# Cross attention of a decoder layer: the product of the maxima ahead of bank 0's in five of sixteen rounds, and the rows' statistics in round 11

## The reference

```python
x = x + _L0_xattn_ref(_layernorm(x, axis=-1), ctx_2048, Wq, bq, Wk, bk, Wv, bv, Wo, bo)
# b = 32, channels 128, 512 positions, 8 heads of 16 channels
q = _apply_rotary(q_emb, split_heads(_proj(x, Wq, bq)))
k = _apply_rotary(k_emb, split_heads(_proj(c, Wk, bk)))
v = split_heads(_proj(c, Wv, bv))
scores = jnp.einsum('bhtc,bhsc->bhts', q, k) / math.sqrt(K_CH)
p_attn = jax.nn.softmax(scores, axis=-1)
out = jnp.einsum('bhts,bhsc->bhtc', p_attn, v)
return _proj(out, Wo, bo)
```

## Time and profile before

| | us |
|---|---|
| median of 3 runs | 3923.88 |
| lowest and highest | 3922.64 and 3927.17 |
| the profiled execution | 3921.74 |
| its span, first to last instruction | 3919.9 |
| PE busy | 3775.1 (96%) |
| DVE busy | 2853.0 (73%) |
| ACT busy | 2340.5 (60%) |
| POOL busy | 1806.4 (46%) |
| mean granted clock of PE | 0.987 |

### The profile page before, as it was taken

One profiled execution on the slowest core, in us unless ns is written; L12 is line 12 of the kernel. 1 busy time (PEld: TensorE's weight loads), 2 busy tenths in 40 slices (PEclk: granted clock), 3 DMA queues, 4 the chain that ended last, 5 costly groups with the idle time before them and its releaser, 6 DMA issues.

```text
span 3919.9 us, 74126 instructions
## 1 busy us (share of the span) xinstructions
PE 3775.1 (96%) x24778; PEld 2974.5 (76%) x24778; DVE 2853.0 (73%) x5969; ACT 2340.5 (60%) x5418; POOL 1806.4 (46%) x2121
## 2 busy tenths in 40 slices
PE   7999999979999999999889999999999999999999
PEld 6888888844444444444389999999999999999998
DVE  5777777657888888888746777777777777877333
ACT  5777777647777777776725555555555555555221
POOL 2222223233555555554424556665666665665210
PEclk9999999979999999999999999999999999999999
DMA  5000000023443333444236999999999999998421
GB/s 203 20 26 23 23 23 23 18 79 109 126 124 121 122 123 122 128 133 143 85 102 197 270 260 267 268 267 264 259 268 267 265 267 267 268 267 235 157 94 60
DMA packets 290168, 621.37 MB, mean 159 GB/s; under 512 B 70000, under 2 KB 78576, under 8 KB 289664
## 3 DMA queue, kind: packets, MB, share of 16 engines
q1 hardware_dynamic: 224640, 464.01, 36.3%
q0 software_dynamic: 64000, 150.52, 15.9%
q10 hardware_dynamic: 1152, 2.10, 0.1%
HBM read 459.93 MB, written 155.98 MB: 157 GB/s over the span
## 4 chain that ended last, share of the span: by engine, by line
PE 85%; DVE 7%; ACT 4%; issue 3%; DMA 1%; SPq 1%; POOL 0%; DVEq 0%; ACTq 0%; POOLq 0%
PE ps L525 20%; PE ps L527 18%; PE ps L526 18%; PE ps L701 6%; PE ps L512 4%; PE ps L662 4%; PE ps L684 4%; PE ps L551 3%; PE ps L624 3%; PE ps L795 2%; PE ps L821 2%; ACT PX L973 2%; DVE WD L1454 1%; DVE NM L1306 1%; PE ps L543 1%
## 5 line engine op out<-in xcount | busy, mean ns | idle before, releaser
L525 PE MATMUL ps<-WG,XT 128*128 128x352 f32 x2304 | 765.4, 332 | 8.0 <-DVE XT L1483 5.4
L526 PE MATMUL ps<-WG,XT 128*128 128x352 f32 x2304 | 744.0, 323 | 0.0
L527 PE MATMUL ps<-WG,XT 128*128 128x352 f32 x2304 | 743.9, 323 | 0.0
L973 ACT ACTIVATE PX<-ps 128x1024 f32<-128x1024 f32 x512 | 523.4, 1022 | 261.1 <-PE ps L684 253.7
L1306 DVE TENSOR_REDUCE NM<-ps 128x2 f32<-128x1024 f32 x512 | 622.5, 1218 | 69.3 <-PE ps L662 65.9
L1800 POOL DMA_INDIRECT sum<-YO,TI x224 | 399.2, 1782 | 495.8 <-issue 392.0
L1447 DVE TENSOR_TENSOR WG<-WL,WG 128x704 fp32r<-128x704 f32 x528 | 450.2, 883 | 30.9 <-ACT WG L1086 30.7
L1119 ACT ACTIVATE HS<-ps 128x352 f32<-128x352 f32 x288 | 133.9, 465 | 559.5 <-PE ps L527 559.5
L1489 DVE TENSOR_TENSOR HS<-ps,HS 128x352 f32<-128x352 f32 x288 | 151.0, 524 | 423.6 <-ACT HS L1119 420.1
L525 PEld LDWEIGHTS ps<-WG,XT 128*128 128x128 f32 x2304 | 433.9, 188 | 9.1 <-DVE XT L1483 6.3
L906 ACT ACTIVATE PA<-ps,nb 128x128 f32<-128x128 f32 x1024 | 360.4, 381 | 131.7 <-DVE nb L1175 131.6
(11 more groups left out here) (275 smaller groups left out, 8677.5 us busy)
## 6 DMA issues: line engine op xcount, KB each, us to landing
WL<-in_w_gate SPq DMA_DIRECT2D x128, 704.0 KB, 4.3
WL<-in_w_up SPq DMA_DIRECT2D x128, 704.0 KB, 5.9
DL<-in_w_down SPq DMA_DIRECT2D x128, 512.0 KB, 8.4
kq_parts<-HL SPq DMA_DIRECT2D x64, 512.0 KB, 3.0
KS<-kq_parts SPq DMA_DIRECT2D x384, 64.0 KB
QS<-kq_parts SPq DMA_DIRECT2D x384, 64.0 KB
DL<-in_w_down SPq DMA_DIRECT2D x128, 192.0 KB, 9.1
CB<-sum POOLq DMA_DIRECT2D x64, 256.0 KB, 3.0
```

What stands on the lines that cost most here:

```text
L525: pe.matmul(out_, lh(0), rh(0), start=first, stop=False)
L526: pe.matmul(out_, lh(0), rh(1), start=False, stop=False)
L527: return pe.matmul(out_, lh(1), rh(0), start=False, stop=last)
L973: act.activation(PX[:, n % 4, :, :], ps[:, 5 * 512:7 * 512], ACT.Exp, scale=0.25).then_inc(S["a_px"], 1)
```

## The change

A tuple `FIRST` names five rounds: 0, 11, 12, 13 and 14. In these, `top(n)` stands ahead of the step on bank 0; in the others behind it, as before. This holds for PE (the product) and DVE (the reduction) alike. And `stats_m(b + 2)` is called in round 11, as its first step behind the round's products, and no longer in round 9 ahead of `stack`. Nothing is computed differently, and no wait is added or removed.

```diff
+FIRST = (0, 11, 12, 13, 14)
...
     if 0 <= n - LAG < 16 * NB:
         do("score", n - LAG)
+    if r in FIRST and 0 <= n < 16 * NB:
+        do("top", n)
     do(*{0: ("keys_of", b, 0), 1: ("maxima", b - 1, 1), 2: ("rotate", b + 1, 0, 0), 3: ("rotate", b + 1, 0, 1),
...
-    if 0 <= n < 16 * NB:
+    if r not in FIRST and 0 <= n < 16 * NB:
         do("top", n)
...
     if r == 9:
         do("high", b + 1, 1)
         do("low", b + 1, 1)
-        do("stats_m", b + 2)
         do("stack", b + 1, 0, 0)
...
     if r == 11:
+        do("stats_m", b + 2)
         do("away", b + 1, 1)
```

## The result

| | kernel before | changed kernel |
|---|---|---|
| median (lowest to highest) | 3926.47 us (3922.64 to 3927.58), 6 runs | 3940.22 us (3935.45 to 3950.07), 6 runs |
| profiled execution, span | 3921.74 us, 3919.9 us | 3940.55 us, 3938.7 us |
| mean granted clock over the span | 0.987 | 0.984 |

The changed kernel is slower: the ratio is 1.0041, with a 95% interval of 1.0027 to 1.0055. Forecast were 3931.1 us, within 3920 to 3939.

A forecast was written before the change was run, and what follows sets the result against it. TensorE was taken to bound the cross-attention block. Profiled 3921.74 us plus 29 blocks at +.25 us (7.3) gave 3929.0; with 2.1 for the median over the profiled run, 3931.1 us, range 3920 to 3939.

The forecast's parts named there:

- X11: `turn_g` of round 11 on TensorE: starts .43 us later because `top` of round 11 now stands ahead of it.
- T13 to G: Spacing on TensorE from `top` of round 13 to `gate`, start to start: .33 us.
- S13 to the `apply` of round 1: TensorE from `score` of round 13 to round 1's `apply`: bound by its own work, .18 us shorter.
- the pause before S13: TensorE stands .5 us before `score` of round 13, waiting for the exponential on ScalarE; before the change .2.
- TensorE's waits for PX: TensorE's waits for the exponential's output, summed over the blocks: up by about 9 us.
- XB's wait: VectorE's wait for `join`'s product: falls from 1.8 us to under .6, worth nothing on TensorE.
- The rule on mode changes: Score of round 13 to round 1's `apply`: 12 tiling-mode changes become 11, .10 us for one; kernel about 3933.4 us.
- What comes back from S13 on: From `score` of round 13, TensorE regains part of the .43 us delay: .18, leaving +.25 per block.
- 3921.74 + 7.3: Whole kernel: profiled time before plus 29 blocks (3 to 31) at .25 us each, giving 3929.0 us.
- Rival 1: Full-width products behind a pair (`gate`, `join`, `keys_of`) need .10 more: +.55 us per block, 3939.8 us, chance .20.
- Rival 2: ScalarE isn't late, round 12's exponential keeps its place: block .28 us shorter, 3915.8 us, chance .07.
- Rivals 3 and 4: VectorE bounds some rounds, 3914.4 us, chance .04; a later TensorE wait for ScalarE swallows the .25, 3923.9, chance .12.

The follow-up runs named there:

- e2: Changed kernel with the old order in every round, only the statistics still moved to round 11: 3928.54 us, ratio .9999 to the kernel before.
- e4: Changed kernel with `top` first in round 11 alone: 3951.00 us, ratio 1.0052 to the kernel before.
- e3: Changed kernel with round 11 taken out of the list, `top` first in 0, 12, 13 and 14: 3925.18 us, ratio .9992 to the kernel before.
- e7: Changed kernel with the copy to OS (`high_o`, with `low_o`) moved from round 11 to 12: 3924.25 us, ratio .9997 to the kernel before.
- e8: Kernel before with the copy to OS (`high_o`, with `low_o`) moved from round 11 to 12: 3921.37 us, ratio .9988.
- e9: Changed kernel without round 11 in the list and with the copy to OS in round 12: 3921.25 us, ratio .9983 to the kernel before.
- e10: As e9, and `high`/`low` of (b + 1, 1) moved from round 9 to 10: 3916.63 us, ratio .9976 to the kernel before.
- e6: Changed kernel with the new order only in blocks 0 to 2 and 28 to 31: 3929.16 us, ratio 1.0011 to the kernel before.
- e11: Changed kernel with `top`'s two products issued three times in round 12 to fill TensorE's pause: 3938.01 us, ratio 1.0032 to the kernel before.
- e12: Changed kernel with the new order only from block 1 on: 3936.72 us, ratio 1.0028 to the kernel before.
- e13: Changed kernel with the new order only from block 3 on: 3937.19 us, ratio 1.0031 to the kernel before.
- e14: As e10, with the new order only from block 3 on: 3914.42 us, ratio .9971 to the kernel before.
- after_again: Changed kernel measured once more without an edit, in a second group: 3937.86 us, ratio 1.0035 to the kernel before.

## Why the prediction was wrong, point by point

**Right, with its size:** what bounds the block. X11 slips by .44 (forecast .43), T13 to G is .33, G to A 1.01, S13 to the `apply` of round 1 9.24 (forecast 9.24), the pause before S13 .46 to .49 (forecast .5), the period +.245 (forecast +.25). TensorE's waits for PX rose by 12.9 us, where I had said about 9, because the whole .46 is new in the view: S13 had no recorded wait before (the pair ahead of it is drawn up to its start), and 29 x .46 = 13.3. XB's wait fell under .6 (23 of at most .4); six others come to 3.4 together, the longest 1.7. norm_m follows PX of round 13 without a gap. The statistics are worth nothing (e2).

**The rule on mode changes.** What comes back from S13 on was .18 (34.72 in e4, 34.54 in the changed kernel) and not .10: a pair behind a pair lasts .40 against .50, and what stands behind it starts .33 against .43 later. The Trainium skill, "TensorEngine Tiling (Array Packing)", Key Properties, is right that a change of mode costs, but counting the changes at .10 each gives too little back here; its estimate, 3933.4 us, is nearer to the measured time for a reason that has nothing to do with it.

**The step that failed** is the first sentence of the sum: 3921.74 + 7.3. It takes everything outside the 29 blocks' mechanism, the granted clock above all, as unchanged, and so puts blocks 0 to 2, where the order changes too, at nothing. Three things were missing from it.
1. The base. The median of the kernel before over six runs is 3926.47, not 3923.88; in the other groups it lay from 3925.65 to 3928.69. That is 2.6 of the 9.1 us between forecast and result, and no matter of the change.
2. The clock. It is .984 and .987 in the two profiled executions. Over all executions of this study (the kernel before, the changed one and 14 more) a line through time and mean clock, with a constant for each kernel, has a slope of 2.3 us for each .001. The mean clock of the changed kernel's 12 executions is .0011 to .0018 lower than before's, which gives 2.5 to 4 us. Part of it is the longer time at 1.2 GHz in blocks 0 to 2, shown in eleven traces above (2.6 and 2.9 us in the changed kernel's two).
3. At equal clock, by the same line, the changed kernel stands 8.0 and 11.0 us (its two groups) above the kernel before, some 9.5, and the blocks account for 7.1. About 2 us are not assigned.

The second group's median, 3937.86, lies inside the forecast's range, and the first lies 1.2 us outside, less than the two differ. So that the range was just missed is in part chance; that 5 to 7 us beyond the block's 7.1 were missing is not: the lower ends of the two intervals are 10.6 and 9.0 us.

My views were the stretch 1200 to 1600, where the clock is 1.00. The clock of the first 40 us and of the last 200 us of cross attention would have shown that the time isn't the block's period times the blocks: .66 and .97 there.

**The rivals.** Rival 1 named 3939.8, .4 from the measured median. It is refuted all the same: its deciding point was T to G above .38, and that is .33, in the changed kernel and in e3; its +.55 per block is .245. A number that fits is no evidence for its cause. Rival 2 (ACT isn't late) falls by the 1.08 us that ACT idles before x3T, and by e7. Rivals 3 and 4 fall by the period. The chances had .46 for a time within .2% and .43 for a slower one; slower came. A range that ended at 3939 left no room for an unpriced term of several us on top of the forecast.

**The expectations of the experiments** held for every block period to .05 but e8's (34.11 expected, 34.00 measured). They missed in whole times, in both directions: e4 (more lost, by dips in the clock), e3, e7, e9 and e10 (less gained), e6 (3.5 us lost, where the block gave 1 and the rival at least 5), e11 (no gain), e12 (no cure), e13 (a cure at the head, none of the whole), e14 (12 us gained of 13 to 15).

**What stays open.** Why the new order in blocks 0 to 2 brings more time at 1.2 GHz; why the pause before S13 is followed by a dip in some blocks and not in others (after_again has one in the middle, the first profiled execution none); whether the dips near the end belong to a kernel or to a run; the 2 us above. In the changed kernel's first profiled execution one standstill near the end remains without a cause:

```profile
1907.97 1.06 PE L705 MATMUL ps<-PX,vh 128*32 128x512 f32 x8
...
1909.84 0.63 PE L516 MATMUL ps<-CST,ox 128*128 128x128 f32 x4 [0.80 <-issue]
1910.37 1.02 ACT L977 ACTIVATE PX<-ps 128x1024 f32<-128x1024 f32 x1 [3.04 <-remote]
```

ACT idles 3.04 us before an exponential whose product had started at 1907.55, and nothing in the profile names what it waited for.

## What to carry to other kernels

When a step moves on the busiest engine, follow its reader through the in-order engine behind it: here the price of one pair put ahead was set by a copy that stood in ScalarE's queue between two others, and moving that copy was worth more than any order on TensorE. An idle stretch of an engine that nobody waits for is not a gain to be had, however large its number. And a sum of block periods is only a forecast of the time if the granted clock at the ends of the stage and in the middle is part of it; give it a term, or at least its width in the range.

## What the runs showed of the hardware

In cross attention with TensorE about 95% busy the granted clock still falls for short times to 1.2 GHz; a block that is touched once takes 36.1 us in place of 34.54. In the seven traces with a pause of TensorE in round 12 or 13 that nothing fills, such falls came 0 to 4 times from 940 to 1760 us, each in round 13 behind the pause; in e11, where the pause of .46 us is filled, none came, and the median stayed (3938.01 against 3937.86). Over the whole kernel .001 of mean clock goes with 2.3 us. And two kernels that differ only in where five rounds have `top`, and that in the first three blocks, are 2.8 to 3.1 us apart there (e13 and the changed kernel, -.2 against 2.9 and 2.6), at a clock of .86 against .82 and .83.
